# A selective-scan stage laid out anew: states and channels together on the partitions, a convolution inside a projection, inputs spread by DMA

## The reference

```
xz   = norm(x2) @ in_proj_w.T;  x, z = split(xz)          # 512 tokens x 512 each
u    = silu(conv4(x) + conv_b)                            # causal, 4 taps, per channel
dt, B, C = split(u @ x_proj_w.T)                          # 16, 16, 16
delta = softplus(dt @ dt_proj_w.T + dt_b)
h[d,n](t) = exp(-delta[d](t)*exp(A_log[d,n])) * h[d,n](t-1) + delta[d](t)*u[d](t)*B[n](t)
y[d](t)   = sum over n of h[d,n](t)*C[n](t),  plus D[d]*u[d](t)
out  = (y * silu(z)) @ out_proj_w.T + quantised(norm(x2)) @ quantised(W).T + bias + x2
```

## Time and profile before

| | us |
|---|---|
| median of 3 runs | 2258.15 (2257.34 to 2266.96) |
| profiled execution | 2259.47 |
| its span | 2257.7 |
| PE, DVE, ACT, POOL busy | 1794.6, 1582.8, 963.1, 1052.2 |

### The profile page before, as it was taken

One profiled execution on the slowest core, in us unless ns is written; L12 is line 12 of the kernel. 1 busy time (PEld: TensorE's weight loads), 2 busy tenths in 40 slices (PEclk: granted clock), 3 DMA queues, 4 the chain that ended last, 5 costly groups with the idle time before them and its releaser, 6 DMA issues.

```text
span 2257.7 us, 20924 instructions
## 1 busy us (share of the span) xinstructions
PE 1794.6 (79%) x6312; PEld 844.5 (37%) x6312; DVE 1582.8 (70%) x1836; ACT 963.1 (43%) x1480; POOL 1052.2 (47%) x740
## 2 busy tenths in 40 slices
PE   7489899989899989894368877787777777877876
PEld 7253535353535353531123423433234233342333
DVE  6456464646464646452598898988979889889895
ACT  3125252626252525352437346364363643735532
POOL 2600000000000000004878959879598796896962
PEclk9899999999999999996689988999899998999999
DMA  5553536253526262602402204003031040210400
GB/s 179 205 80 109 92 101 100 101 96 106 93 98 103 94 107 94 107 10 82 159 0 81 98 1 159 19 32 128 19 142 37 1 158 19 99 70 2 149 10 9
DMA packets 84205, 189.13 MB, mean 84 GB/s; under 512 B 10561, under 2 KB 62914, under 8 KB 72370
## 3 DMA queue, kind: packets, MB, share of 16 engines
q1 hardware_dynamic: 81074, 180.07, 29.0%
q0 software_dynamic: 3072, 8.37, 1.2%
HBM read 151.72 MB, written 36.70 MB: 83 GB/s over the span
## 4 chain that ended last, share of the span: by engine, by line
DVE 14%; PE 11%; POOLq 11%; POOL 10%; issue 6%; ACT 1%; DVEq 1%; ACTq 0%
DVE ps L1372 6%; PE ps L1481 6%; DVE work L1378 3%; POOLq L1120 3%; POOL work L1148 3%; POOLq L1196 2%; POOL xn L1124 2%; PE ps L1461 2%; DVE u L1363 2%; POOLq L1139 2%; POOLq L1137 2%; PE ps L1489 2%; POOL e_rows L1122 1%; DVE absmax L1345 1%; POOL e_rows L1083 1%
## 5 line engine op out<-in xcount | busy, mean ns | idle before, releaser
L1481 PE MATMUL ps<-work,ident_sb 128*128 128x512 f32 x1024 | 548.0, 662 | 210.5 <-DVE work L1378 209.9
L1148 POOL TENSOR_TENSOR work<-bc,du 128x1024 f32<-128x1024 f32 x256 | 601.4, 2361 | 181.3 <-PE ps L1481 179.4
L1372 DVE TENSOR_TENSOR_SCAN ps<-ps,work 128x1024 f32<-128x1024 f32 x256 | 585.4, 2287 | 93.9 <-ACT ps L1257 50.4
L1257 ACT ACTIVATE ps<-delta,a_neg 128x512 f32<-128x512 f32 x512 | 331.7, 682 | 318.3 <-DVE work L1378 317.6
L699 DVE TENSOR_REDUCE m<-ps 128x1 f32<-128x512 f32 x512 | 327.3, 685 | 164.0 <-PE ps L805 162.3
L1481 PEld LDWEIGHTS ps<-work,ident_sb 128*128 128x128 f32 x1024 | 200.1, 208 | 500.0 <-DVE work L1378 321.1
L622 ACT ACTIVATE prob<-ps 128x1024 f32<-128x1024 f32 x256 | 256.8, 1021 | 234.5 <-PE ps L829 232.3
L1378 DVE TENSOR_TENSOR work<-ps,bc 128x1024 f32<-128x1024 f32 x256 | 308.4, 1205 | 0.0
L563 POOL TENSOR_TENSOR m_parts<-m,nil 128x16 bf16<-128x16 f32 x32 | 7.1, 221 | 604.2 <-DVE m L699 604.2
L805 PE MATMUL ps<-k_st,q_st 96*128 96x512 bf16 x512 | 184.5, 407 | 59.0 <-DMA k_st<-qk_parts 36.9
L1461 PE MATMUL ps<-xn_t,in_w 128*128 128x512 f32 x256 | 142.0, 688 | 54.0 <-DVE u L1363 35.1
(11 more groups left out here) (168 smaller groups left out, 2045.3 us busy)
## 6 DMA issues: line engine op xcount, KB each, us to landing
bc<-bc_rows SPq DMA_DIRECT2D x64, 1024.0 KB, 4.7
w<-in_w SPq DMA_DIRECT2D x32, 1024.0 KB, 8.6
qk_parts<-parts SPq DMA_DIRECT2D x96, 128.0 KB
q_st<-qk_parts SPq DMA_DIRECT2D x96, 128.0 KB, 10.5
k_st<-qk_parts SPq DMA_DIRECT2D x96, 128.0 KB, 11.3
dispatch<-zeros SPq DMA_DIRECT2D x4, 1280.0 KB, 10.6
x_in<-in_x SPq DMA_DIRECT2D x8, 512.0 KB, 3.6
rows<-dispatch SPq DMA_DIRECT2D x32, 128.0 KB, 7.3
```

What stands on the lines that cost most here:

```text
L1148: nc.gpsimd.tensor_tensor(work[:, n % WS, :, :], bc[:, j, 0, :, :], du[:, b % 2, c, :].unsqueeze(1).broadcast_to([P, PAIR, SEQ]), ALU.mult ...
L1257: e = nc.scalar.activation(state(n)[:, i, :], delta[:, b % 2, c, :], ACT.Exp, scale=a_neg[:, c, PAIR * j + i:PAIR * j + i + 1])
L1372: nc.vector.tensor_tensor_scan(s, s, work[:, n % WS, :, :].rearrange("p i t -> p (i t)"), 0.0, ALU.mult, ALU.add).then_inc(state_ready, 1)
L1481: x = nc.tensor.matmul(ps[:, YB, :], sb["ident"][:, :], work[:, n % WS, i, :], start=False, stop=(n % PAIRS == PAIRS - 1 and i == PAIR - 1))
```

## The change

All of it is in `mix_block` and its inputs.

- **Layout.** A piece is now 4 states x 32 channels on the partitions (`QUADS` = 4 groups of `CH` = 32), and two blocks of 32 channels along the row. There are still 32 pieces of 128 x 1024 elements for a sequence. One quad of states k and a half h name a piece inside a chunk.
- **Sums.** PE multiplies by `pick` (128 x 32, four identities of 32 on top of each other), which sums four states in the contraction; the result of each block of channels goes to its own 32 partitions of YB. Two pieces are summed in one go, four matmuls. `WS` goes from 6 to 4.
- **Convolution.** The projection's weights are multiplied once by each tap (`tap_weights`), and the four products with shifted inputs are accumulated in PSUM: 8 matmuls per chunk instead of 2, and no DVE work.
- **Spread.** delta and delta*u of a chunk (`inputs`) go to DRAM and come back as `rep`, once for each of the four partition groups. B and C rows go to 32 partitions each.
- **Moved to ACT.** Weighing the experts, normalising, and two scalings of the quantisation step. The grid steps on POOL go from 5 to 3. The gathers for sequence f+1 are issued one sequence earlier.
- **Strides.** `absmax` has a stride of two elements, and the clamp of `xn_step` is walked with a stride of two.
- The tables are new, since the work stands at other pieces.

```diff
-WS = 6
+WS = 4
-GRID_STEPS = 5
+GRID_STEPS = 3
-PE_AT = {"out": 2, "w": 2, "first_quant": (3, 4), "turn_x": (10, 11), "x": (12, 13, 14, 15), "bc": 18, "dt": (19, 20, 21, 22),
+PE_AT = {"out": (1, 3), "w": 1, "first_quant": (3, 4), "turn_x": (6, 7), "x": (8, 10, 12, 14), "bc": 17, "dt": (19, 20, 21, 22),
          "z": (23, 24, 25, 26), "turn_quant": (27, 28)}
-ACT_AT = {"out": (6, 10), "w": 3, "first_quant": (4, 5), "turned": (11, 12), "x": (13, 14, 15, 16), "silu_u": 18, "bc": 19,
-          "dt": (20, 21, 22, 23), "softplus": 24, "z": (24, 25, 26, 27), "quant": (28, 29), "silu_z": 29}
+ACT_AT = {"out": (4, 6), "w": 2, "first_quant": (4, 5), "weigh": 0, "normalise": 6, "turned": (8, 9), "x": (11, 13, 15, 17), "silu_u": 17,
+          "step": 13, "rows": 19, "dt": (21, 22, 23, 24), "softplus": 24, "z": (25, 26, 27, 28), "quant": (29, 30), "silu_z": 30}
-POOL_AT = {"gather": 0, "weigh": 3, "add": 4, "root": 10, "normalise": 11, "down": 16, "grid": 22, "up": 27, "input": 28}
+POOL_AT = {"add": 1, "root": 5, "down": 10, "grid": 15, "up": 18, "gather": 20, "input": 27}
...
+                def load_inputs(f, c):
+                    sp.wait_ge(rep_stored[c], f * 16 + 16)
+                    if f:
+                        n = (f - 1) * PIECES + (c + 1) * PER_CHUNK
+                        sp.wait_ge(decay_ready, n)
+                        sp.wait_ge(drive_ready, n)
+                    for i in range(QUADS):
+                        sp.dma_start(rep[i * CH:(i + 1) * CH, c, :, :, :].rearrange("p j r t -> p j (r t)"),
+                                     io["rep"][f % 2, c].rearrange("(j p) x -> p j x", p=CH)).then_inc(rep_loaded[c], 16)
+
+                def spread(f):
+                    store_rows(f)
+                    store_inputs(f, 0)
+                    store_inputs(f, 1)
+                    load_inputs(f, 0)
+                    store_inputs(f, 2)
+                    load_inputs(f, 1)
+                    load_quad(f, 0)
+                    store_inputs(f, 3)
+                    load_quad(f, 1)
+                    load_inputs(f, 2)
+                    load_quad(f, 2)
+                    load_quad(f, 3)
+                    load_inputs(f, 3)
...
                 def drive(b, q):
+                    if q % PER_CHUNK == 0:
+                        pool.wait_ge(rep_loaded[c], (b + 1) * QUADS * 16)
+                    if c == 0 and h == 0:
+                        pool.wait_ge(bc_loaded[k], (b + 1) * QUADS * 16)
                     if n >= WS:
-                        pool.wait_ge(summed, n - WS + 1)
-                    nc.gpsimd.tensor_tensor(work[:, n % WS, :, :], bc[:, j, 0, :, :],
-                                            du[:, b % 2, c, :].unsqueeze(1).broadcast_to([P, PAIR, SEQ]), ALU.mult).then_inc(drive_ready, 1)
+                        pool.wait_ge(summed, (n - WS) // 2 + 1)
+                    nc.gpsimd.tensor_tensor(work[:, n % WS, :, :], rep[:, c, 2 * h:2 * h + 2, 1, :],
+                                            bc[:, k, 0, :].unsqueeze(1).broadcast_to([P, 2, SEQ]), ALU.mult).then_inc(drive_ready, 1)
...
+                def in_proj_taps(bank, c, done):
+                    for s in range(TAPS):
+                        for k in range(KD):
+                            x = nc.tensor.matmul(ps[:, bank, s:], in_x[:, k, TAPS - 1 - s, c * P:(c + 1) * P], xn_t[:, k, 0:SEQ - s],
+                                                 start=(s == 0 and k == 0), stop=(s == TAPS - 1 and k == KD - 1))
+                    x.then_inc(done, 1)
...
+                def sum_states(k):
+                    pe.wait_ge(read_ready, 2 * k + 2)
+                    for n in (2 * k, 2 * k + 1):
+                        for i in range(2):
+                            j = 2 * (n % 2) + i
+                            x = nc.tensor.matmul(ps[j * CH:(j + 1) * CH, YB, :], pick[:, :], work[:, n % WS, i, :],
+                                                 start=False, stop=(n % PER_CHUNK >= PER_CHUNK - 2))
                     x.then_inc(summed, 1)
...
-                        if q % PAIRS == 1:
-                            seed(b, q // PAIRS)
                         n = b * PIECES + q
-                        if n:
-                            sum_states(n - 1)
+                        if q % PER_CHUNK == 2:
+                            seed(b, q // PER_CHUNK)
+                        if n and n % 2 == 0:
+                            sum_states(n // 2 - 1)
```

More of the change, by code:

```diff
@@ L967, in mix_block @@
         fw_step = sz[:, 1, 1, :].rearrange("p (h c) -> p h c", h=2)
-        xn_step = e_rows[:, :, :].rearrange("p (h t) c -> p h (t c)", h=2)
+        xn_step = e_rows
+        conv_rows = work[:, 0:2, :, :].rearrange("p a i t -> p (a i) t")
+        nudge = inputs[:, DC - 1, :, :].rearrange("p r (t d) -> p (r t) d", d=DM)
+        delta, du = inputs[:, :, 0, :], inputs[:, :, 1, :]
         const_loaded = sem("const_loaded3")
@@ L1055, in _ @@
                 load(2)
-                spread(0, False)
+                spread(0)
                 for b in range(BATCH + 1):
@@ L1064, in _ @@
                     if b + 1 < BATCH:
-                        spread(b + 1, True)
+                        spread(b + 1)
                 sp.wait_ge(out_stored, BATCH * 16)
@@ L1303, in _ @@
                             silu_u(f)
-                        if q == ACT_AT["bc"]:
+                        if q == ACT_AT["step"]:
+                            scale_step(f)
+                        if q == ACT_AT["rows"]:
                             copy_rows(f, TB)
@@ L1362, in convolve, with tap_weights @@
+                def tap_weights():
+                    dve.wait_ge(const_loaded, CONSTS * 16)
+                    raw = in_x[:, :, TAPS - 1, :]
+                    for tap in range(TAPS):
+                        if tap == TAPS - 1:
                             dve.drain()
-                        r = nc.vector.scalar_tensor_tensor(u[:, f % 2, c, s:], ps[:, bank, 0:SEQ - s], conv_w[:, c, k:k + 1],
-                                                           u[:, f % 2, c, s:], ALU.mult, ALU.add)
@@ L1475, in seed @@
                         pe.wait_ge(y_ready, b * DC + c)
-                    nc.tensor.matmul(ps[:, YB, :], d_diag[:, c, :], u[:, b % 2, c, :], start=True, stop=False)
-                def sum_states(n):
-                    pe.wait_ge(read_ready, n + 1)
-                    for i in range(PAIR):
-                        x = nc.tensor.matmul(ps[:, YB, :], sb["ident"][:, :], work[:, n % WS, i, :],
-                                             start=False, stop=(n % PAIRS == PAIRS - 1 and i == PAIR - 1))
+                    nc.tensor.matmul(ps[:, YB, :], d_diag[:, c, :], u[:, (b * DC + c) % US, :], start=True, stop=False)
@@ L1495, in out_proj @@
-                    if t % 2:
-                        x.then_inc(out_done, 1)
+                        for k in range(KD):
+                            nc.tensor.matmul(o, quant_t[:, b % 2, k, t * P:(t + 1) * P], fw_t[:, k, :], start=False, stop=False)
+                        nc.tensor.matmul(o, one_row, bias, start=False, stop=False)
+                        x = nc.tensor.matmul(o, sb["ident"][:, :], x2[:, b % XS, t, :], start=False, stop=True)
+                    x.then_inc(out_done, 1)
                 def turn_weights():
@@ L1616, in layer_kernel @@
     io["bc"] = nc.dram_tensor("bc_rows", (2, 2 * NS, SEQ), F32, kind="Internal").ap()
+    io["rep"] = nc.dram_tensor("rep_rows", (2, DC, P, 2 * SEQ), F32, kind="Internal").ap()
     io["x1"] = nc.dram_tensor("x1", (BATCH, P, TT, DM), F32, kind="Internal").ap()
```

319 lines of the change are left out of this document (168 added, 151 removed).

## The result

| | before | after |
|---|---|---|
| median, us | 2257.74 (4 runs, 2256.93 to 2266.96) | 2563.05 (4 runs, 2561.65 to 2564.64) |
| span of the profiled execution | 2257.7 | 2562.8 |
| mean granted clock | 0.926 | 0.801 |

The ratio is 1.1343, with a 95% interval of 1.1325 to 1.1361. The forecast was 2422 with 2300 to 2475: the direction was right, the size was not, and the measured time lies 88 us above the range. Both kernels agree within their own runs to 0.5%.

The account below looks back on a forecast made before the run. DVE bounds the old kernel; the change adds waits from a short ring and the spread. First scan 1144.4, sequence 0 156.5, six of 162.7, and the last sequence make 2420, plus 1.8: 2422 us, range 2300 to 2475.

Parts of the forecast that it names:

- the start: Ahead of the mixer's first scan: more projection matmuls, POOL's preparation and a 27.8 us spread put it at 1144.4, was 1102.9.
- The loop of a pair: Ring of four buffers, per pair of pieces: scan, read, sum of 1.07, drive; 7.1 us against 6.6 of DVE.
- Pieces 0 to 8: Half output projections of 7.9 us on PE ahead of each of two sums; T(8) = 34.6 us.
- The taps: Pieces 8 to 16: folded convolution's 6.9 us blocks on PE ahead of sums; 44.6 us, not 28.4, 16.2 lost.
- The clock: Rival: after longer idle between sequences PE runs the output projection at a low granted clock; 4 us a sequence, 2450; chance 0.13.
- Pieces 16 to 24: POOL's grid steps, scaling and gathers stand ahead of drives; from T(16) = 79.2 to T(24) = 114.2 us.
- 24 to 26: Late z copy puts the second z projection ahead of sum(22,23) on PE; T(26) = T(24) + 12.9 = 127.1 us.
- The boundary: Between sequences, the first drive waits for queued spread transfers at 262 GB/s; next first scan at T(26) + 35.6 us.
- 2452: Time if 32-partition loads at the boundaries run at the skill page's 218 GB/s; each boundary 3.7 us longer.
- Faster: Rival: PE and POOL blocks fit between sums, loads run at 431 GB/s; 124 us a sequence, about 2144; chance 0.07.
- The fast spread: Rival: spread loads run at the rate of 128 partitions; 7.0 us less at eight places, 2366; chance 0.15.
- The hidden blocks: Rival: the convolution's PE blocks hide in room left by ACT and PE's order; 16.2 x 7 less, 2309; chance 0.12.

## Why the forecast had the sign and not the size

The forecast of the span, 2420.3 by its terms, is 142.5 us short of the profiled 2562.8: the start 10.6 (1155.0, not 1144.4); sequence 0 17.2 (173.7, not 156.5); the six in the middle 98.8 (1075.0, not 976.2); the last one and its tail 15.9 (159.1, not 143.2).

The mechanism was right: a ring without spare puts PE's blocks on the path, and each boundary waits for transfers. Two sizes in the sum failed. PE's sums, blocks and output tiles were entered with durations of the full clock (1.07, 6.9 and 1.89 us) and ran in good part at half of it (1.94, up to 10.14 and 3.78); and the loads to 32 partitions were entered at 262 GB/s and ran at 202 to 216. Of the 18.0 us that the third sequence is longer than forecast the first explains some 10 and the second some 6; the rest is 2.2 in pieces 16 to 26.

- **The loop of a pair** was to take 7.1 us, with a sum of 1.07. It takes 8.0 in the last sequence, with a sum of 1.94. The eight records of the earlier trace rows stand in the attention part, where PE was at 9 tenths and its clock at 9; in the last sequence PE's only work for long stretches is this sum, and its clock is 0.50. The step that failed is that a duration was carried from a stretch at one clock to a stretch at the other. The filler behind the sums shows it. In the other sequences half of the sums are at 1.07.
- **Pieces 0 to 8** took 37.5 us, forecast 34.6; two sums of 1.94 us and a first output tile of 3.78 us instead of 1.89 stand in that stretch, 3.6 us in all; no run took them away.
- **The taps**, 44.6 us forecast, 51.8 measured, +7.2. The mechanism was as described, block, seed, sum and gate in that chain; the blocks were taken at 6.9 and last 7.1 to 10.1, which alone is 8 us (35.6 against 27.6). Here too it is the clock, as far as the windows show: each block that follows a wait for ACT has a stretch at 0.50 in it, and the one block that didn't wait lasts 7.12. The clock was listed as a rival, but at the output projection, at 4 us a sequence. It is worth some 2 there, and it acts at half of the sums and at three of four blocks as well.
- **Pieces 16 to 24** took 35.9, forecast 35.0; **24 to 26** 14.2, forecast 12.9. The first is right, the second 1.3 short.
- **The boundary** was to take 35.6 us from T(26) and takes 41.3. The chunks were ready and the stores landed nearly as forecast: store 1 landed 13.9 us behind T(26), forecast 13.3 (which by its own terms, 10.8 and 2.9, should have read 13.7). What failed is the rate: load 0 was through at 25.4 and not at 21.3, load 1 at 37.3 and not at 30.6, at 202 to 216 GB/s and not at 262. The 262 was twice the rate of 16 partitions. The Trainium skill, page "SBUF — State Buffer", section "Door 1: The DMA port swizzle", states about 218 for 32 partitions. Here trace and page agree, the windows showing 202 to 216, and 218 with the rest of the prediction's sum would have given its 2452, an estimate still 111 short of the median.
- **The start** was 10.6 late. 3.9 of it are the part ahead of the mixer, which ended at 1023.3 us and not at 1019.4; its end spreads that much over all the kernels here, so this need not come from the change. The first chunk's inputs were ready at 1122.2, forecast 1116.6, so 1.7 more; and the spread took 32.8 us instead of 27.8, at the low rate. The products of the tap weights were to be hidden, and were not:

```profile
1041.78 2.34 POOL L1126 TENSOR_TENSOR x<-x,e_rows 128x1024 f32<-128x1024 f32 x1 [6.60 <-ACT e_rows L1236]
...
1043.62 5.14 DVE L1432 TENSOR_TENSOR in_taps<-in_taps,work 128x1024 f32<-128x1024 f32 x4 [17.99 <-DMA rows_w<-in_fbias]
...
1048.79 1.40 DVE L1396 BATCH_NORM_STATS2 stats<-x 128x6 f32<-128x256 f32 x4
```

  The rows were complete at 1044.12, and the statistics stood 4.7 us behind the products. With half of the products (the kernel with six buffers) they stood 2.4 behind, and PE's first block came 32.3 us after the part ahead instead of 34.7. In the sum it doesn't show, since weighing and normalising, which moved to ACT, take 1.70 and 2.07 us there instead of 3.64 and 4.85 on POOL: before, that stretch took 35.5.
- **The rivals.** Faster was to be decided by whether PE's blocks can begin well ahead of the read that they delay. They couldn't in this order; with the sums first, or with eight buffers, they can. The fast spread did not occur; loads at full width gave 70, forecast 56. The hidden blocks did not occur. That DVE would be under 75% in the mixer held: it is at 62%. Half of the sums were at the 1.07 us that the prediction wanted to see.

What is shown: the ring (some 190 us by two more buffers), the place of the sum in PE's list (105), the order of the spread (105), the rate (70). They are not to be added: ring and list give the same time twice, and order and rate both shorten the wait at the boundary. The clock's share is shown in the last sequence alone (0.86 us a pair); in the taps and the output tiles it is read from the windows, and no experiment took it away there.

## What to carry to other kernels

Count a ring in units of what frees it: four buffers freed in pairs are two, and then a block ahead of the freeing instruction is on the path unless it began early (three of the four here were). Put that instruction first in its engine's list before you take work out. A duration from another stretch has a clock with it: look up the granted clock where the row stands and where the work will stand. And check a transfer's place in its queue as well as its rate.

## What the runs showed of the hardware

- Where most of a block's work was taken from PE, the rest ran at the low level: with one tap, two matmuls took 3.78 us in three of four blocks, with four taps the high level was reached inside the block. Work added (four matmuls behind each sum) made the chain shorter: scan 31 of the last sequence came at 121.5 us instead of 129.0.
- 18 matmuls of filler that end 3.6 us ahead of the work gave nothing: the sum behind them took 1.94 us again.
- Loads of 0.5 MB to 32 partitions moved 202 to 216 GB/s with all DMA engines full, although four of them, to four different quarters of the partitions, were queued together; the same bytes to 128 partitions moved 418.
- Four f32 matmuls of 32 columns, each to its own quarter of the PSUM partitions, take 1.07 us at the full clock and 1.94 at the low one, where one f32 matmul of 128 columns takes 0.86.
